# Mixer: conv and gate projections as three float32r products, gate in 512-token tiles half a sequence ahead

## The reference, cut to what matters

```python
proj = jnp.einsum('bsd,ed->bse', x, in_proj_w)          # x is the layer norm of the input
gate = proj[..., :INTER]
hBC  = proj[..., INTER:INTER + CONV_DIM]                # hidden channels, B and C
xc   = conv1d(hBC, conv_w, causal, 4 taps) + conv_b
hBC  = silu(xc)
...                                                     # decays, Y_diag, states, Y_off by chunk and head
g    = y * silu(gate)
gg   = g grouped by 1024 channels;  gg *= rsqrt(mean(gg * gg) + EPS)
out  = (gg * norm_w) @ out_proj_w.T
x    = x + out
```

## Time and profile before

| | |
|---|---|
| median of 3 runs | 2969.13 us |
| profiled execution | 2967.0 us, its span 2965.2 us |
| TensorE matmul (PE) | 2758.0 us busy, 93% |
| TensorE weight load (PEld) | 1805.8 us, 61% |
| VectorE (DVE) | 1940.1 us, 65% |
| ScalarE (ACT) | 1129.7 us, 38% |
| GpSimd (POOL) | 593.5 us, 20% |
| DMA | 155.94 MB, mean 53 GB/s |

### The profile page before, as it was taken

The page is one execution under the profiler, slowest core; times in us unless marked ns, Lnnn a source line. Parts: engine busy times, 40 slices in busy tenths (PEclk is TensorE's granted clock), DMA queues, the critical chain, the costliest instruction groups (busy, mean ns, idle before and its releaser), DMA issues. The chain is left out here.

```text
span 2965.2 us, 42961 instructions
## 1 busy us (share of the span) xinstructions
PE 2758.0 (93%) x15936; PEld 1805.8 (61%) x15936; DVE 1940.1 (65%) x3087; ACT 1129.7 (38%) x2241; POOL 593.5 (20%) x512
## 2 busy tenths in 40 slices
PE   3699999999999999999999999999698889999899
PEld 2266666666766666666676666667586444444388
DVE  5566777677677677767767767775554646666364
ACT  1333434344343343434434334342221336666421
POOL 1222132221213213222121321222221001111031
PEclk7799999999999999999999999999798989999999
DMA  4211121121112212112211212301101401111000
GB/s 147 62 35 39 46 88 38 43 91 44 37 59 73 39 46 88 38 42 92 44 38 60 72 38 47 88 20 23 75 0 74 164 29 40 38 38 36 1 11 18
DMA packets 128562, 155.94 MB, mean 53 GB/s; under 512 B 29344, under 2 KB 89840, under 8 KB 125680
## 3 DMA queue, kind: packets, MB, share of 16 engines
q1 hardware_dynamic: 122912, 151.34, 18.0%
q10 hardware_dynamic: 5456, 2.00, 0.3%
HBM read 134.93 MB, written 18.38 MB: 52 GB/s over the span
## 5 line engine op out<-in xcount | busy, mean ns | idle before, releaser
L455 PE MATMUL bank<-xnT,wh 128*128 128x512 f32 x1280 | 573.7, 599 | 29.4 <-issue 26.2
L741 DVE SCALAR_TENSOR_TENSOR cacc<-raw,cwh,cacc 128x512 f32<-128x512 f32 x480 | 421.8, 880 | 221.4 <-ACT cacc L726 210.0
L549 PE MATMUL bank<-xnT,wg 128*128 128x128 f32 x4096 | 480.1, 275 | 0.0
L549 PEld LDWEIGHTS bank<-xnT,wg 128*128 128x128 f32 x4096 | 467.3, 192 | 3.3 <-issue 3.3
L592 PE MATMUL bank<-wo,yt 128*128 128x512 f32 x1024 | 453.0, 595 | 7.9 <-DVE yt L839 7.9
L455 PEld LDWEIGHTS bank<-xnT,wh 128*128 128x128 f32 x1280 | 236.7, 191 | 296.7 <-issue 288.5
L592 PEld LDWEIGHTS bank<-wo,yt 128*128 128x128 f32 x1024 | 193.6, 190 | 247.6 <-issue 247.6
L651 ACT COPY xs<-bank 128x512 f32<-128x512 f32 x128 | 74.5, 582 | 414.7 <-PE bank L481 414.7
L1981 DVE TENSOR_REDUCE at_nm<-bank 128x1 f32<-128x512 f32 (+3 forms) x256 | 150.3, 589 | 109.3 <-PE bank L1847 89.2
L934 POOL TENSOR_TENSOR rr<-rr,nhalf 128x1 f32<-128x1 f32 x64 | 35.2, 549 | 914.0 <-DVE rr L872 914.0
L1945 ACT ACTIVATE at_PT<-bank 128x512 f32<-128x512 f32 (+3 forms) x384 | 167.4, 498 | 118.2 <-PE bank L1860 114.0
(11 more groups left out here) (240 smaller groups left out, 4393.5 us busy)
## 6 DMA issues: line engine op xcount, KB each, us to landing
wh<-w_hs_dram SPq DMA_DIRECT2D x160, 256.0 KB, 2.7
EC<-ecum_scratch SPq DMA_DIRECT2D x112, 256.0 KB, 8.3
wg<-w_gate_dram SPq DMA_DIRECT2D x8, 2048.0 KB, 8.1
wo<-w_out_dram SPq DMA_DIRECT2D x8, 2048.0 KB, 8.9
qk_scratch<-at_part SPq DMA_DIRECT2D x48, 256.0 KB
at_qT<-qk_scratch SPq DMA_DIRECT2D x32, 192.0 KB, 2.6
at_kT<-qk_scratch SPq DMA_DIRECT2D x32, 192.0 KB, 2.7
wgu<-w_gu_dram SPq DMA_DIRECT2D x1, 3584.0 KB, 11.2
```

The costliest lines, as they stand in the source:

```text
L455: mm = nc.tensor.matmul(BA[bank][:, :], wh[:, i % WR, k, :], xnT[:, k, h * HALF:(h + 1) * HALF], start=(k == 0), stop=(k == KC - 1))
L549: mm = nc.tensor.matmul(BA[b][:, i * P:(i + 1) * P], wg[:, k, j * P:(j + 1) * P], xnT[:, k, ttok], start=(k == 0), stop=(k == KC - 1))
L741: nc.vector.scalar_tensor_tensor(dst, raw[:, r, 2 - k:2 - k + HALF], w(2 - k), dst, ALU.mult, ALU.add)\
```

## The change

Both projections take split operands, and the gate is computed like the conv tiles: 128 channels for 512 tokens, for the next half.

- **Input.** The setup block writes `xh`, the normalized input as float32r, beside `xnT` (one more ScalarE copy a chunk), and GpSimd makes the rest `xl = xnT - xh`. `xnT` lives in the setup block only.
- **Weights.** Each tile of either kind (18 a half: eight gate, ten conv, in the order `TILES`) is loaded into one of three raw buffers, two of which are `xn`'s. ScalarE copies it to `wh` (float32r, `ac_high`), VectorE subtracts for `wl` (`dv_low`), both in rings of three, three tiles ahead of use. There are 16 halves, so 288 tiles. The load of tile `q + 3` waits for `dv_low` of `q`.
- **Products.** `pe_tile` does `wh*xh + wh*xl + wl*xh`: 12 float32r matmuls of 512 columns for each tile.
- **Order.** A slot with a successor half holds two gate tiles, in the places of `u = 0` and `1`, beside its 4, 3, 3 or 0 conv tiles. The prologue holds the 18 tiles of the first half. The gate goes to `G2`, which holds one half. `yt` is multiplied by it right after the diagonal output is added, ahead of the small copies. The last four slots have no projection at all.
- **Buffers.** `wg`, `st1` and the use of `xn` for squares go; the squares use `xs`, and their ScalarE instruction now waits until `xch` of the next chunk is made. GpSimd scales `st` in place.

```diff
-        WR = PT // 2
-        xnT = sb(ctx, "xnT", [P, KC, T])
+        RR, WR = 3, 3
+        TILES = [t for c, (lo, hi) in enumerate(SHARE)
+                 for t in [("gate", 2 * c), ("gate", 2 * c + 1)] + [("conv", i) for i in range(lo, hi)]]
...
+        xh = sb(ctx, "xh", [P, KC, T], F32R)
+        xl = sb(ctx, "xl", [P, KC, T], F32R)
...
-        wg = sb(ctx, "wg", [P, KC, GC])
+        rawx = sb(ctx, "rawx", [P, KC, P])
+        wh = sb(ctx, "wh", [P, WR, KC, P], F32R)
+        wl = sb(ctx, "wl", [P, WR, KC, P], F32R)
...
+        raws = [rawx[:, :, :]] + [xn[:, r, :].rearrange("p (k m) -> p k m", k=KC) for r in range(2)]
...
+            sp.dma_start(raws[q % RR], src.rearrange("o p k m -> p (o k) m")).then_inc(d_raw[q % RR], 16)
...
-                        nc.scalar.copy(xnT[:, :, z * P:(z + 1) * P],
-                                       BANK[z % 2][:, :].rearrange("p (k t) -> p k t", k=KC)).then_inc(ln_xt, 1)
+                        for dst in (xnT, xh):
+                            nc.scalar.copy(dst[:, :, z * P:(z + 1) * P],
+                                           BANK[z % 2][:, :].rearrange("p (k t) -> p k t", k=KC)).then_inc(ln_xt, 1)
...
+                    for z in range(NT):
+                        cols = slice(z * P, (z + 1) * P)
+                        pool.wait_ge(ln_xt, 2 * (z + 1))
+                        nc.gpsimd.tensor_tensor(xl[:, :, cols], xnT[:, :, cols], xh[:, :, cols], ALU.subtract).then_inc(p_ch, 1)
...
+        def pe_tile(pe, p, kind, i, bank):
+
+            q = number(p, kind, i)
+            s, tok = q % WR, slice(p[1] * HALF, (p[1] + 1) * HALF)
+            dv_lo.wait(pe, q + 1)
             for k in range(KC):
-                mm = nc.tensor.matmul(BA[bank][:, :], wh[:, i % WR, k, :], xnT[:, k, h * HALF:(h + 1) * HALF],
-                                      start=(k == 0), stop=(k == KC - 1))
+                for m, (w, x) in enumerate(((wh, xh), (wh, xl), (wl, xh))):
+                    mm = nc.tensor.matmul(BA[bank][:, :], w[:, s, k, :], x[:, k, tok],
+                                          start=(k == 0 and m == 0), stop=(k == KC - 1 and m == 2))
...
             for u in range(2):
-                release_a(pe, g, z, u)
-                b = bank()
-                for i in range(4):
-                    j = 4 * u + i
-                    for k in range(KC):
-                        mm = nc.tensor.matmul(BA[b][:, i * P:(i + 1) * P], wg[:, k, j * P:(j + 1) * P], xnT[:, k, ttok],
-                                              start=(k == 0), stop=(k == KC - 1))
-                mm.then_inc(pe_gt.sem, 1)
+                if step:
+                    release_a(pe, g, z, u)
+                    pe_tile(pe, step, "gate", 2 * (z % CH) + u, bank())
...
+        def ac_high(act, q):
+
+            if q >= LAST_TILE:
+                return
+            act.wait_ge(d_raw[q % RR], 16 * (q // RR + 1))
+            pe_P.wait(act, q - WR + 1)
+            nc.scalar.copy(wh[:, q % WR, :, :], raws[q % RR]).then_inc(ac_hi.sem, 1)
+
+        def ac_gate_tanh(act, p, j, bank):
+            q = number(p, "gate", j)
+            m = (2 * p[0] + p[1]) * JT + j
+            dv_sg.wait(act, m - 1)
+            pe_P.wait(act, q + 1)
+            nc.scalar.activation(sg[:, j % 2 * 512:(j % 2 + 1) * 512], BA[bank][:, :], ACT.Tanh, scale=0.5)\
+                .then_inc(ac_tg.sem, 1)
+            ac_high(act, q + WR)
...
             nc.scalar.activation(cacc[:, m % CR, :], ps[:, :], ACT.Identity, bias=cwh[:, h, j, TAPS:TAPS + 1],
                                  scale=cwh[:, h, j, TAP:TAP + 1]).then_inc(ac_raw.sem, 1)
+            ac_high(act, q + WR)
...
+        def dv_low(dve, q):
+
+            if q >= LAST_TILE:
+                return
+            ac_hi.wait(dve, q + 1)
+            pe_P.wait(dve, q - WR + 1)
+            nc.vector.tensor_tensor(wl[:, q % WR, :, :], raws[q % RR], wh[:, q % WR, :, :], ALU.subtract).then_inc(dv_lo.sem, 1)
+
+        def dv_gate_tile(dve, p, j, bank, gated):
...
+            nc.vector.scalar_tensor_tensor(gate_tile(p, j), t3(sg[:, j % 2 * 512:(j % 2 + 1) * 512]), 1.0,
+                                           t3(BA[bank][:, :]), ALU.add, ALU.mult).then_inc(dv_sg.sem, 1)
+            dv_low(dve, number(p, "gate", j) + WR)
...
+            nc.vector.tensor_tensor(yv, yv, gate_chunk(h, c), ALU.mult).then_inc(dv_gg.sem, 1)
             if mine and not last:
                 dv_small(dve, *nxt)
...
-            nc.vector.tensor_tensor(yt[:, :], yt[:, :], sg[:, :], ALU.mult).then_inc(dv_gg.sem, 1)
...
             def conv(r):
                 if r < len(mine):
                     bank()
+                    dv_low(dve, number(step, "conv", mine[r]) + WR)
                 if r < len(mine) - 1:
                     dv_conv_tile(dve, step, mine[r])
...
-                    pe_P.wait(sp, (2 * p[0] + p[1]) * PT + i + 1)
+                    dv_lo.wait(sp, q + 1)
                     sp.sem_inc(turned, 1)
-                    load_tile(sp, p[0] + (p[1] if i >= WR else 0), (i + WR) % PT)
+                    load_tile(sp, q + RR)
...
-                    pe_gt.wait(sp, 2 * (8 * g + 8))
-                    load_gate(sp, g + 1)
```

More of the change, by code:

```diff
@@ L200, in _ @@
                             .then_inc(s_x[i], 16)
[L202 to L204 removed]
+                    load_tile(sp, 0)
                     load_out(sp, 0)
+                    sp.wait_ge(ln_ps, NT)
+                    for q in range(1, RR):
+                        load_tile(sp, q)
                     sp.wait_ge(v_ch, 22)
@@ L568, in tile @@
                 if r < 2:
-                    dv_sg.wait(pe, 2 * n + r + 1)
+                    dv_sg.wait(pe, gates_done(n, r))
                 else:
                     ac_raw.wait(pe, RAW * ((2 * step[0] + step[1]) * PT + mine[r] - 1))
-                pe_tile(pe, step, mine[r], bank())
+                pe_tile(pe, step, "conv", mine[r], bank())
             if not last:
@@ L649, in ac_xs_copy @@
             dv_xc.wait(act, n)
+            dv_sq.wait(act, n - 1)
             pe_hs.wait(act, 2 * n + u + 1)
@@ L694, in ac_slot @@
             dv_sq.wait(act, n)
+            if not last:
+                dv_xc.wait(act, n + 2)
             nc.scalar.activation(sq, yt[:, :], ACT.Square).then_inc(ac_sq.sem, 1)
@@ L715, in ac_tile_copy @@
             dv_cv.wait(act, TAP * (m - 1))
-            pe_P.wait(act, m + 1)
+            q = number(p, "conv", i)
+            pe_P.wait(act, q + 1)
             if h == 0:
@@ L1012, in slot_loads @@
                     step, mine = tiles_of(g, z)
-                    for i in mine:
-                        next_tile(step, i)
+                    if step:
+                        for kind, i in [("gate", 2 * (z % CH)), ("gate", 2 * (z % CH) + 1)] + [("conv", i) for i in mine]:
+                            next_tile(number(step, kind, i) + WR)
                     if end:
@@ L1052, in prologue @@
                 def prologue(bank):
-                    for i in range(PT):
-                        ac_raw.wait(pe, RAW * (i - 1))
-                        pe_tile(pe, (0, 0), i, bank())
+                    for q, (kind, i) in enumerate(TILES):
+                        if q >= 2:
+                            was, w = TILES[q - 2]
+                            if was == "gate":
+                                dv_sg.wait(pe, w + 1)
+                            else:
+                                ac_raw.wait(pe, RAW * (w + 1))
+                        pe_tile(pe, (0, 0), kind, i, bank())
                     pe_pre(pe, 0, 0)
@@ L1065, in prologue @@
                     act.wait_ge(s_set, 5)
-                    for i in range(PT):
+                    for q in range(WR):
+                        ac_high(act, q)
+                    for kind, i in TILES:
+                        if kind == "gate":
+                            ac_gate_tanh(act, (0, 0), i, bank())
+                            continue
                         TILE_BANK[(0, i)] = bank()
@@ L1078, in prologue @@
                     dve.wait_ge(s_set, 5)
-                    for i in range(PT):
-                        bank()
+                    for q in range(WR):
+                        dv_low(dve, q)
+                    for kind, i in TILES:
+                        b = bank()
+                        if kind == "gate":
+                            dv_gate_tile(dve, (0, 0), i, b, 0)
+                            continue
+                        dv_low(dve, number((0, 0), "conv", i) + WR)
                         dv_conv_tile(dve, (0, 0), i)
@@ L1087, in prologue @@
                     dv_masked(dve, 0, 0)
-                run(dve, dv_slot, prologue, (dv_cv, dv_act, dv_sm, dv_xc, dv_M, dv_yo, dv_yd, dv_sg, dv_gg, dv_st, dv_out, dv_r, dv_sq))
+                run(dve, dv_slot, prologue, (dv_lo, dv_cv, dv_act, dv_sm, dv_xc, dv_M, dv_yo, dv_yd, dv_sg, dv_gg, dv_st, dv_out, dv_r, dv_sq))
     if debug is not None:
```

129 lines of the change are left out of this document (69 added, 60 removed).

## The result

The changed kernel takes 2936.07 us in the median of 4 runs (2932.77 to 2937.45), beside 2968.64 us for the kernel before (4 runs, 2967.29 to 2969.56): a ratio of 0.9889, 95% interval 0.9872 to 0.9906. It is faster by 32.6 us. 2858 us was forecast, 110.5 us faster; the range, 2775 to 2935, missed the time by 1 us.

What follows compares the result with a forecast made beforehand. TensorE was taken as the bound, with VectorE's chain level with it at slot ends. 198 - 36 - 7 - 7 - 39 - 24 - 3.5 + 29 = 110.5 us saved gave 2858 us, range 2775 to 2935.

Steps and rivals of the forecast that it cites:

- What the change takes from TensorE: Shorter conv and gate products in 60 slots with a successor half, 13.2 us a set of four: +198 us.
- The three-tile slots: At the slot's end TensorE waits 1.2 us for VectorE's reduction, in 30 slots: -36 us.
- T: End of a slot's first conv tile on TensorE, from which the prediction counted the steps at the slot's end.
- The tile-less slots: Later relu and early gating of `yt` make them 22.8 us where products alone give 22.35; 15 slots: -7 us.
- First slot of a group: GpSimd's `wo` multiply blocks VectorE's subtraction; 5.6 us charged in each of 7 groups: -39 us.
- Four-tile slots: At the slot's end TensorE is at T + 15.7, VectorE at 16.6; eight slots: -7 us.
- Last four slots: Without gate parts they take 66 us in place of about 95: +29 us.
- Prologue and setup: Copy and subtraction enter the prologue's conv loop, gate tiles are added: -24 us; setup's first pieces and copies: -3.5 us.
- the 60 slots of the sum: Slots with a successor half, 15 sets of four with 10 conv and 8 gate tiles, over which +198 us was counted.
- rival 3: VectorE's taps and subtractions leave a backlog carried into the next slot: 2933 us, from 2900 to 2965; chance 0.23.
- Rival 1: VectorE keeps up, so the four losses in the slots, 89 us, do not occur: 2769 us; chance 0.17.
- Rival 4: Weight pieces come late and `pe_tile` waits on `dv_lo`: slower, 3067 us with half the prologue's excess; chance 0.07.

Runs made afterwards that it cites:

- n4: Changed kernel, with VectorE taking the leftover tile's silu and first gate product ahead of `xch` in slots with conv tiles: 2882.93 us.
- n3: Changed kernel, with the first gate tile's subtraction moved behind the state and `BC` in slots without conv tiles: 2900.39 us.
- n13: Changed kernel, with seven unread float32r matmuls added where TensorE waits for `BC`, in 15 slots without conv tiles: 2923.73 us.
- n10: Changed kernel, with the multiply of `wo` in a group's first slot moved from GpSimd to ScalarE: 2916.01 us.
- n1: Changed kernel, with the subtraction cut to one column and the third product using the weights' high piece again: 2881.77 us.
- n11: Changed kernel with first pieces ahead of memsets, gate product ahead of `xch`, tile-less subtraction behind `BC`, taps ahead of subtraction, `wo` multiplied by ScalarE: 2806.23 us.
- n12: n11 plus, in the prologue, ScalarE copying a conv tile ahead of the previous tile's tanh and VectorE's taps ahead of its subtraction: 2789.67 us.
- n2: Changed kernel, with ScalarE and VectorE making the first three high and low pieces before waiting for GpSimd's memsets: 2932.03 us.

## Why the prediction was wrong, step by step

The direction was right and every price of an operation held; the size was off by 78 us, and what failed is the walk through the waits inside a slot. By the spans before and after, 31 us were gained where 110.5 were forecast; the 79 missing are these.

- **What the change takes from TensorE: right.** 0.232 from start to start was forecast, 0.227 to 0.232 measured, so the +198 us stand as TensorE's saving. The new copy takes 0.62 us, 0.51 from start to start (0.55 was taken), and the subtraction 0.68 where nothing holds it, as was taken.
- **The three-tile slots, the largest miss.** "Counted from T, the end of the slot's first conv tile on TensorE" is the sentence that failed. It lets TensorE come to T on its own time and walks only what lies behind. What lies ahead of T on VectorE and ScalarE (leftover taps, tanh, high copy, `xs` copy, `xch`, gate product) ends 1.4 us too late for TensorE. This place had 1.55 us of slack before; the shorter products took about as much from one side and `yt*G` and the high copy, both ahead of the gate product, from the other. The prediction priced no wait there. Slots became 33.00 - 31.69 = 1.3 us shorter in place of 2.44 (three tiles at 0.68 and two gate parts at 0.80, less 1.2): 34 us over 30 slots. n4 shows the cause, as the order alone gives back 1.6 us a slot. The part that I did walk was about right (0.94 for 1.2).
- **The tile-less slots.** "I get 22.8": I charged a later relu, and put nothing down for `BC` behind a subtraction that `hd` holds, though I had used that same block for the first slot. They became 23.77 in the mean, longer than before (23.15), for a forecast gain of 1.15: 15 x (1.15 + 0.62) = 27 us. n3 shows it, by removing 2.0 and 2.9 us.
- **The clock.** Every term was priced at the full clock, and the earlier trace rows had nothing else to show. Between slots of one kind in the kernel after, one with a fall takes some 1.4 us more than one without (at z = 3, behind the same wait of 1.7 us, five with a fall take 24.45 to 24.76 us and two without 23.29). 19 falls more than before make about 27 us; this is no further item but a part of the others: 12 falls lie in tile-less slots (17 of their 27 us), 6 in first slots. n13 shows it: 12 us less, with TensorE's own work starting no earlier.
- **First slot of a group: right.** 35 forecast, 35.36 measured; the blocked subtraction was to last "up to 7 us" and lasts 6.91, TensorE's bank was to come 3 us late and comes 2.84 late. n10 removes the block and shows that ScalarE's own work is close behind. The Trainium skill ("SBUF — State Buffer", Who interferes with whom: the later of the two instructions is fully blocked) is borne out by the 6.91 and the 0.69 us.
- **Four-tile slots: 32.4 forecast, 32.6 measured.** 3 us over seven slots; the first slots take another 3 or 4.
- **Last four slots:** 66 forecast, 67.2 measured; 1 to 2 us.
- **Prologue and setup.** The conv tile's loop was forecast at 5.56 us and is 5.44; from the first tile to the first `sqs` it takes 122.5 us in place of 98.5, the 24 forecast. The setup was put at 3.5 and costs 9.2, as the first pieces wait for the memsets. Some 4 us more are a matter of counting: group 0's own first slot was in the 60 slots of the sum, and its block kept that gain from coming. Together 10 us.

34 + 27 + 3 + 3.5 + 1.5 + 10 = 79.

**The rivals.** The time lies beside rival 3, *VectorE becomes the bound* (2933 us), and its mechanism is not the one at work. VectorE is busy for 1557 of 1893 us, and n1, which takes its new load away, leaves the largest wait where it was. In the three-tile slot above VectorE waits for TensorE at the start (0.47 us ahead of `rr`), so no backlog is carried over; what the rival names rightly is that `hd` and the leftover taps stand ahead of what TensorE needs. n11 keeps the whole load and runs 130 us faster. Rival 1, *VectorE keeps up*, gave 2769 us; n11, with the order in the slots mended, comes to 2806, and n12, with the prologue's too, to 2790. Rival 4 did not happen: of all waits in the slot stretch only GpSimd's for `wo` ends with a DMA, and TensorE's only long wait for `wl` is the first tile's. What would have warned: the forecast had VectorE finishing level with TensorE at the end of a slot, and the same comparison was owed for each of TensorE's other waiting points, the first conv tile's bank and `BC`.

Still open: how the 3.3 us that n2 gives back divide, and why the same wait of 1.7 us at z = 3 is followed by a fall of the clock in five slots and by none in two.

## What to carry to other kernels

When a change shortens one engine's work by a tenth, list every point where this engine waits for another inside one period, and compare the arrival times at each of them, not only at the end. In each in-order queue, look for the operation that the bound engine needs and move it ahead of those that only refill rings or serve the next period; here such moves, with one multiply given to another engine, brought 130 us where the change itself had brought 33. Price a wait of TensorE with what the clock did behind waits of its length in the trace, here another 1.4 us in most of the slots without tiles.

## What the runs showed of the hardware

The granted clock. Behind TensorE's wait of 2.24 us in the slot shown, and of 2.84 in the first slot of a group, it fell to 1.2 GHz 1.0 to 2.0 us after the wait had ended, for 3.4 us in most cases; the waits of 0.94 and 1.45 us in the three-tile slots went with 1.00 in 29 of 30 slots. It cost some 1.4 us each time. Its consequences were larger than expected: with a third fewer projection matmuls the kernel was 13 us slower (71 falls), and with 105 unread matmuls more it was 12 us faster (7 falls in place of 20). GpSimd's `hd` took 2.85 us in place of 1.90 when VectorE's `yt*G` was running at its start, and three taps that overlapped it 3.56 in place of 2.32. A VectorE subtraction of 0.68 us took 6.91 while GpSimd's multiply of `wo` ran, and 0.69 in the same place when ScalarE made that multiply.
